# A three-step gated graph network on 64 graphs: host-laid inputs, one accumulating gate bank in two copies, and a new order in the first frame

## The reference

```
a  = A h                      (the same A for "in" and "out")
z  = sigmoid(W3 [a, a] + b_w3 + U3 h + b_u3)
r  = sigmoid(W4 [a, a] + b_w4 + U3 h + b_u3)
hv = tanh(W5 [a, a] + b_w5 + U5 (r * h) + b_u5)
h  = (1 - z) * h + z * hv
```

## Time and profile before

| | |
|---|---|
| median of 3 runs | 770.13 us (769.85 to 770.3) |
| the profiled execution | 770.7 us, of it the span 768.7 us |
| mean granted TensorE clock | 0.992 of full speed |
| PE busy | 752.5 us (98%), 3722 matmuls |
| DVE, ACT, POOL busy | 612.0, 438.8, 67.3 us |
| DMA | 52.15 MB in 285234 packets, 267386 of them under 512 B |

### The profile page before, as it was taken

The page is one execution under the profiler, slowest core; times in us unless marked ns, Lnnn a source line. Parts: engine busy times, 40 slices in busy tenths (PEclk is TensorE's granted clock), DMA queues, the critical chain, the costliest instruction groups (busy, mean ns, idle before and its releaser), DMA issues.

```text
span 768.7 us, 10991 instructions
## 1 busy us (share of the span) xinstructions
PE 752.5 (98%) x3722; PEld 637.8 (83%) x3722; DVE 612.0 (80%) x969; ACT 438.8 (57%) x745; POOL 67.3 (9%) x91
## 2 busy tenths in 40 slices
PE   7999999999999999999999999999999999999994
PEld 6888888888888888888888888888888888888883
DVE  3787688868997778787988777888789867888785
ACT  3565555556766555555666655555567655555564
POOL 0000012100000011110010001120000000211003
PEclk9999999999999999999999999999999999999997
DMA  7811642122265372222156336222225632221223
GB/s 188 144 29 28 104 76 38 30 37 40 39 130 123 66 131 42 32 39 40 29 114 118 71 76 120 38 37 33 37 39 117 138 64 38 32 32 32 43 36 112
DMA packets 285234, 52.15 MB, mean 68 GB/s; under 512 B 267386, under 2 KB 284420, under 8 KB 285188
## 3 DMA queue, kind: packets, MB, share of 16 engines
q1 hardware_dynamic: 284916, 51.24, 35.8%
q10 hardware_dynamic: 272, 0.26, 0.1%
HBM read 18.95 MB, written 8.39 MB: 36 GB/s over the span
## 4 chain that ended last, share of the span: by engine, by line
PE 95%; DVE 2%; DMA 1%; issue 1%; ACT 1%; POOL 0%; ACTq 0%; SPq 0%; POOLq 0%; DVEq 0%
PE ps_a L353 11%; PE ps_uz L328 11%; PE ps_uz L329 11%; PE ps_uz L330 11%; PE ps_v L328 11%; PE ps_v L330 11%; PE ps_v L329 11%; PE ps_r L328 6%; PE ps_r L330 6%; PE ps_r L329 6%; DMA x_in<-in_x 1%; PE ps_uz L426 0%; DVE dz L647 0%; DVE hT L657 0%; DVE stats L757 0%
## 5 line engine op out<-in xcount | busy, mean ns | idle before, releaser
L519 ACT ACTIVATE ps_v<-ps_v,bias 128x512 f32<-128x512 f32 x96 | 63.6, 662 | 73.0 <-PE ps_v L330 73.0
L642 DVE TENSOR_TENSOR dz<-ps_v,hT 128x512 f32<-128x512 f32 x64 | 44.2, 691 | 76.4 <-ACT ps_v L519 76.4
L543 ACT ACTIVATE ps_r<-ps_r,bias 128x512 f32<-128x512 f32 x96 | 63.5, 662 | 71.1 <-DVE ps_r L663 70.2
L514 ACT COPY u_sb<-ps_uz 128x512 f32<-128x512 f32 x96 | 56.4, 587 | 73.5 <-PE ps_uz L330 73.5
L501 ACT CAST aT_hi<-ps_a 128x512 fp32r<-128x512 f32 x96 | 56.1, 586 | 65.5 <-PE ps_a L353 65.4
L328 PE MATMUL ps_uz<-hT_hi,wt_lo 128*128 128x512 f32 x192 | 79.1, 412 | 0.0
L552 ACT CAST rh_hi<-rh 128x512 fp32r<-128x512 f32 x96 | 59.6, 621 | 28.2 <-DVE rh L668 28.2
L329 PE MATMUL ps_uz<-hT_lo,wt_hi 128*128 128x512 f32 x192 | 75.1, 391 | 0.0
L330 PE MATMUL ps_uz<-hT_hi,wt_hi 128*128 128x512 f32 x192 | 75.0, 391 | 0.0
L328 PE MATMUL ps_uz<-aT_hi,wt_lo 128*128 128x512 f32 x192 | 74.9, 390 | 0.0
L328 PE MATMUL ps_r<-aT_hi,wt_lo 128*128 128x512 f32 x192 | 74.9, 390 | 0.0
(11 more groups left out here) (84 smaller groups left out, 1564.8 us busy)
## 6 DMA issues: line engine op xcount, KB each, us to landing
hn<-hb SPq DMA_DIRECT2D x736, 32.0 KB, 2.0
x_in<-in_x SPq DMA_DIRECT2D x16, 512.0 KB, 5.0
x_blk<-in_x SPq DMA_DIRECT2D x64, 128.0 KB, 3.7
out<-y SPq DMA_DIRECT2D x15, 512.0 KB, 3.0
wide<-in_L_gnn_w_w SPq DMA_DIRECT2D x3, 512.0 KB, 4.2
out<-y SPq DMA_DIRECT2D x2, 256.0 KB, 2.1
square<-in_L_gnn_u_w ACTq DMA_DIRECT2D x1, 256.0 KB, 3.3
square<-in_L_gnn_u_w SPq DMA_DIRECT2D x1, 256.0 KB, 4.6
```

Source lines behind the costliest of these rows:

```text
L514: nc.scalar.copy(u_sb[:, oc, :], ps_uz[:, oc, :]).then_inc(u_copied, 1)
L519: nc.scalar.activation(ps_v[:, oc, :], ps_v[:, oc, :], ACT.Tanh, bias=bias[:, BV, oc:oc + 1]).then_inc(v_ready, 1)
L543: nc.scalar.activation(ps_r[:, oc, :], ps_r[:, oc, :], ACT.Sigmoid, bias=bias[:, BR, oc:oc + 1]).then_inc(r_ready, 1)
L642: nc.vector.tensor_tensor(dz[:, c, :], ps_v[:, c, :], h_of(j)[:, c, :], ALU.subtract).then_inc(d_ready, 1)
```

## The change

- The host hands over other layouts: `x` nodes first and also features first, the adjacency and all weights transposed, the biases as one features-first array; the output is written nodes first and turned on the host. PE's 22 transposes of weights, adjacency and biases go, and so do `load_blocks`, `transpose_x` and their buffers. `xT` is loaded directly (`load_cols`, 512 KB in runs of 2 KB).
- `xT` of the next round is loaded by SP right behind `move` of the slot's last frame (frames 8 to 11); before, `load_blocks` stood in `load`, ahead of `load_rows`.
- u, W4 a and then (W3 - W4) a are accumulated in one bank pair `ps_g[j % 2]`: sigmoid(u + W4 a) is read for r between them, and the third product turns the sum into u + W3 a for z. `copy_u` and `add_u` go. The sigmoid for r writes to SBUF (`r_sb`). W3 - W4 is made once (`subtract_r`).
- PE's frame order becomes `gate_r`, `value`, `gate_z`; `gate_z` waits for the sigmoid of r, and `u_product` waits for the z of two frames before, not one. On ACT the two `rh_hi` casts come before the two z sigmoids; on DVE `times_r` comes before `h_low`.
- The first frame has its own order on all engines (`first=True`), 24 and 8 warm-up transposes in place of 10 and 26, and x and weights loaded in another order.

```diff
 (SP)
-            def load_blocks(i, q):
-                for f in range(QUADS):
-                    sp.dma_start(x_blk[q % 2][f * BLK:(f + 1) * BLK, :, :, :],
-                                 x_blocks[f, :, :, bass.ds((SLOTS * i + q) * NBLK, NBLK), :])\
-                      .then_inc(blocks_loaded[q % 2], DMA)
+            def load_cols(i, q, c=slice(0, C)):
+                sp.dma_start(xT[q][:, c, :], x_cols[:, bass.ds(SLOTS * i + q, 1), c, :].rearrange("p g c r -> p (g c) r")).then_inc(xT_loaded[q], DMA)
...
             def load(i, q):
                 oi, oq = (i, q - 2) if q >= 2 else (i - 1, q + 2)
-                sp.wait_ge(xT_ready[oq], oi + 1)
-                load_blocks(i, q)
                 sp.wait_ge(a_ready, 2 * frames(oi, oq))
                 load_rows(i, q)
...
                 if carry or j > 0:
-                    move(*frame_before(i, j))
+                    bi, bj = frame_before(i, j)
+                    move(bi, bj)
+                    if refill and bj >= FR - SLOTS:
+                        load_cols(bi + 1, bj % SLOTS)
...
+            sp.dma_start(adjT[:, :], adj_t).then_inc(adjT_loaded, DMA)
             load_rows(0, 0)
-            load_blocks(0, 0)
...
+            for c in range(C):
+                load_cols(0, 0, slice(c, c + 1))
+            load_wide(W4)
+            load_wide(W5)
+            load_wide(W3)
             load_rows(0, 1)
+            load_cols(0, 1)
+            sp.dma_start(square[1][:, :, :], u5_t).then_inc(w_loaded[U5], DMA)
+            load_cols(0, 2)
+            load_cols(0, 3)
 (PE)
-                    dense(ps_uz, U3, oc, hT_hi, hT_lo, True, True).then_inc(u_ready, 1)
+                    dense(ps_g[j % 2], U3, oc, hT_hi, hT_lo, True, False)
...
-                pe.wait_ge(z_ready, C * frames(*frame_before(i, j)))
+                if carry or j >= 2:
+                    pe.wait_ge(z_ready, C * frames(*two_before(i, j)))
...
-                    dense(ps_r, W4, oc, aT_hi, aT_lo, True, True).then_inc(rpre_ready, 1)
+                    dense(ps_g[j % 2], W4, oc, aT_hi, aT_lo, False, True).then_inc(rpre_ready, 1)
...
-                    pe.wait_ge(u_copied, C * frames(i, j) - 1 + oc)
-                    dense(ps_uz, W3, oc, aT_hi, aT_lo, False, True).then_inc(zpre_ready, 1)
+                    pe.wait_ge(r_ready, C * frames(i, j) - 1 + oc)
+                    dense(ps_g[j % 2], W3, oc, aT_hi, aT_lo, False, True).then_inc(zpre_ready, 1)
...
                 gate_r(i, j)
+                value(i, j, carry)
                 gate_z(i, j)
-                value(i, j, carry)
...
-                keep_warm(10)
-                pe.wait_ge(adj_loaded, DMA)
-                nc.tensor.transpose(adj_bank, adj_in[:, :], ident[:, :]).then_inc(adj_transposed, 1)
-                transpose_weight(U3)
-                pe.wait_ge(adjT_ready, 1)
+                keep_warm(24)
+                pe.wait_ge(adjT_loaded, DMA)
                 aggregate(0, 0)
-                keep_warm(26)
+                keep_warm(8)
                 weight_ready(U3)
-                u_product(0, 0, between=transpose_weight)
...
+                u_product(0, 0)
                 weight_ready(W4)
                 gate_r(0, 0)
+                weight_ready(W5)
+                value(0, 0, False)
                 weight_ready(W3)
                 gate_z(0, 0)
...
+                first_half(0, 1, False)
                 weight_ready(U5)
-                first_half(0, 1)
                 candidate(0, 0)
 (ACT, frame)
                 for oc in range(C):
-                    if following:
+                    if following and not first:
                         h_high(*following, oc)
-                    act.wait_ge(rsum_ready, C * frames(i, j) - 1 + oc)
-                    nc.scalar.activation(ps_r[:, oc, :], ps_r[:, oc, :], ACT.Sigmoid,
+                    act.wait_ge(rpre_ready, C * frames(i, j) - 1 + oc)
+                    nc.scalar.activation(r_sb[:, oc, :], ps_g[j % 2][:, oc, :], ACT.Sigmoid,
                                          bias=bias[:, BR, oc:oc + 1]).then_inc(r_ready, 1)
+                    if first and oc == 0:
+                        weight_high(W3)
+                for oc in range(C):
+                    act.wait_ge(rh_ready, C * frames(i, j) - 1 + oc)
+                    nc.scalar.copy(rh_hi[:, oc, :], rh[:, oc, :]).then_inc(rh_hi_ready, 1)
                 for oc in range(C):
                     act.wait_ge(zpre_ready, C * frames(i, j) - 1 + oc)
...
-                    act.wait_ge(rh_ready, C * frames(i, j) - 1 + oc)
-                    nc.scalar.copy(rh_hi[:, oc, :], rh[:, oc, :]).then_inc(rh_hi_ready, 1)
+                if first:
+                    for oc in range(C):
+                        h_high(*following, oc)
+                    weight_high(U5)
 (DVE, frame)
-                add_u(i, j, 0)
-                if before:
                     new_h(bi, bj, 1)
-                add_u(i, j, 1)
                 for c in range(C):
-                    if following:
+                    times_r(i, j, c)
+                    if first and c == 0:
+                        weight_low(W3)
+                    if following and not first:
                         h_low(*following, c)
-                    times_r(i, j, c)
                 rh_low(i, j, 0)
                 rh_low(i, j, 1)
+                if first:
+                    for c in range(C):
+                        h_low(*following, c)
+                    weight_low(U5)
...
+            def subtract_r():
+                dve.wait_ge(wsum_ready, SUMMED[W3] - 1)
+                nc.vector.tensor_tensor(wsum[W3][:, :, :], wsum[W3][:, :, :], wsum[W4][:, :, :],
+                                        ALU.subtract).then_inc(wsum_ready, 1)
```

More of the change, by code:

```diff
@@ L92, in build @@
         neg_half = sb("neg_half", [P, GB])
-        wide = [sb(f"wide{k}", [P, C, 2 * D]) for k in range(3)]
+        wide = [sb(f"wide{k}", [P, 2, C, D]) for k in range(3)]
         square = [sb(f"square{k}", [P, C, D]) for k in range(2)]
@@ L134, in build @@
         dz = sb("dz", [P, C, ROWS])
-        ps_v, ps_uz, ps_a, ps_r = ps("ps_v"), ps("ps_uz"), ps("ps_a"), ps("ps_r")
+        ps_v, ps_a = ps("ps_v"), ps("ps_a")
+        ps_g = [ps(f"ps_g{k}") for k in range(2)]
         def f32(t):
@@ L271, in store, with frame @@
                              y[q % 2][:, :, :]).then_inc(stored[q % 2], DMA)
-            def frame(i, j, carry):
+            def frame(i, j, carry, refill):
                 if j < 2:
@@ L306, in _ @@
                 for j in range(EARLY, FR):
-                    frame(i - 1, j, True)
+                    frame(i - 1, j, True, True)
                 for j in range(EARLY):
-                    frame(i, j, True)
+                    frame(i, j, True, True)
             last = ROUNDS - 1
             for j in range(EARLY, FR - 1):
-                frame(last, j, True)
+                frame(last, j, True, False)
             for q in range(SLOTS - 1):
@@ L355, in aggregate, with u_product @@
                     done.then_inc(a_ready, 1)
-            def u_product(i, j, between=None):
+            def u_product(i, j):
                 pe.wait_ge(hT_hi_ready, C * frames(i, j))
@@ L485, in _ @@
             candidate(last, FR - 1)
+            pe.wait_ge(z_ready, C * frames(last, FR - 2))
             for c in range(C):
                 pe.wait_ge(h_ready, C * frames(last, FR - 1) - 1 + c)
-                output(SLOTS - 1, c, ps_r)
+                output(SLOTS - 1, c, ps_g[0])
         @block.scalar
@@ L509, in h_high @@
                 nc.scalar.copy(hT_hi[:, c, :], h_of(j)[:, c, :]).then_inc(hT_hi_ready, 1)
-            def copy_u(i, j):
-                for oc in range(C):
-                    act.wait_ge(u_ready, C * frames(i, j) - 1 + oc)
-                    nc.scalar.copy(u_sb[:, oc, :], ps_uz[:, oc, :]).then_inc(u_copied, 1)
             def tanh_v(i, j):
@@ L529, in normalise, with frame @@
                                          scale=rstd[q][:, b:b + 1]).then_inc(normed[q], 1)
-            def frame(i, j, carry, following):
+            def frame(i, j, carry, following, first=False):
                 if carry or j > 0:
@@ L618, in statistics @@
                     nc.vector.bn_aggr(meanvar[q][:, b, :], stats[q][:, b, :]).then_inc(meanvar_ready[q], 1)
-            def transpose_x(i, q):
-                dve.wait_ge(blocks_loaded[q % 2], QUADS * DMA * turn(i, q))
-                nc.vector.transpose(xT[q][:, :, :].rearrange("p c r -> p (c r)"),
-                                    x_blk[q % 2][:, :, :, :].rearrange("p c k f -> p (c k f)")).then_inc(xT_ready[q], 1)
             def transpose_blocks(i, j, again):
@@ L680, in h_low, with frame @@
                                         ALU.subtract).then_inc(hT_lo_ready, 1)
-            def frame(i, j, carry, following):
+            def frame(i, j, carry, following, first=False):
                 before = carry or j > 0
```

(10 more changed lines are left out.)

170 lines of the change are left out of this document (67 added, 103 removed).

## The result

| | before | changed |
|---|---|---|
| median of the runs | 770.05 us (4 runs, 769.85 to 770.3) | 763.06 us (4 runs, 762.16 to 763.5) |
| ratio to before, 95% interval | | 0.9908 (0.989 to 0.9925) |
| the profiled execution, its span | 770.7, 768.7 us | 762.16, 760.4 us |
| first U3 h, U3 h of frame (0, 1) | 14.34, 29.71 us | 8.76, 22.63 us |
| from there to the start of DVE's last `v_minus_h` (its first half) | 726.18 us | 725.26 us |

7.0 us less between the medians, and 8.3 us less span between the two profiled executions. The changed one is the fastest of its runs; the same kernel profiled again had a span of 761.3 us and a median of 763.38 over 5 runs. Where the 8.3 us are: 29.71 - 22.63 = 7.08 in the opening, 726.18 - 725.26 = 0.92 up to the last `v_minus_h`, and 0.3 in what follows it.

What follows compares the result with a forecast made beforehand. PE, holding 95% of the last-ending chain, was taken as the bound, so only the edges could gain: 770.7 - 5.15 (opening) - 0.9 (end) = 764.65 us, forecast 764.1 for the median; range of 8 in 10, 762.4 to 767.7.

Steps and rivals of the forecast that it cites:

- The frame: Steady-state rounds: frames stay 15.40 us apart, PE does not wait, and every added wait costs 0.
- gate z on r: New wait of gate z for r's sigmoid in each frame: 1.35 us of margin in the worst frames, cost 0.
- The slower rival: Rounds: xT's refill behind move comes late and stalls PE; 1 us in each of 12 frames gives 776; chance 0.05.
- The landing of xT: Opening: xT of slot 0 lands at 8.6 us, the middle of 6.7 and 10.5.
- PE's own path: Opening: 24 warm-ups, the aggregation and 8 warm-ups end at 10.1 us; the data decides, U3 h starting at 10.65.
- U3 h at 9.3: Opening, early end of the forecast: PE-bound, gain 6.5 us there; with 0.9 at the end, 762.7 us.
- Everything behind it: First frame after U3 h at 10.65: four products, aggregation and a 1.0 us stall, U3 h of (0, 1) at 24.55.
- Two thirds from x and the warm-ups that no longer fill the gap: Opening: two thirds of its 5.15 us gain come from features-first x and those warm-ups, the smaller part from the transposes.
- The end: Last v_minus_h: DVE's statistics start over 1 us earlier and the tanh decides, 0.9 us gained, bounds 0 and 0.95.
- The sum: Whole kernel: 770.7 - 5.15 - 0.9 = 764.65 us, then 0.57 lower for the median, 764.1.
- The clock rival: Opening: PE falls to half clock after idling, costing 1.5 to 2 us, 765.9 us in all; chance 0.08.
- The rival of late loads: Opening: the slowest DMA engine sets each landing, xT at 10.2 and W3 at 17.1 us; 767.3 us; chance 0.16.

Runs made afterwards that it cites:

- e2: The changed kernel with gate z directly behind gate r again, ahead of value; 783.75 us, ratio 1.0178.
- e4: The changed kernel without its 24 and 8 warm-up transposes; 763.27 us, ratio 0.9915.
- e3: The changed kernel with x_in read from the reference's own layout, in runs of 1 KB and not 4 KB; 763.31 us, ratio 0.9925.
- e7: The changed kernel with xT loaded in 128-byte runs, one DMA per chunk, still features first; 765.31 us, ratio 0.994.
- e1: The changed kernel with ACT's two casts of h of frame (0, 1) ahead of the first frame's z sigmoids; 761.97 us, twice.
- e8: e1 with xT of slot 0 loaded ahead of x_in and without the 8 later warm-ups; 767.74 us, ratio 0.9969.
- e9: e8 with 48 warm-ups in front in place of 24; 763.28 us, ratio 0.9916.
- e10: e1 without the 8 warm-ups behind the first aggregation, loads in the changed kernel's order; 765.07 us, ratio 0.9937.
- e6: The changed kernel with the accumulating bank taken back: u copied and added, gate z before value, W3 itself; 765.17 us, ratio 0.9941.

## Why the prediction was right

It forecast 764.1 us and 763.06 was measured, a gain of 7.0 where 6.0 had been worked out. In the second trace, 763.05 us and so near the median, U3 h of (0, 1) comes at 23.52, 1.0 us before the 24.55 forecast, as much as the forecast of the median is off. Step by step:

- **The frame.** 15.40 us and no wait of PE in the rounds, as said, with every added wait at cost 0. The one that I thought nearest, gate z on r, was the nearest: 1.49 us of margin against 1.35 forecast, and e2 shows its price when the margin is gone, 19 us of span and 20 in the medians. The slower rival (xT's refill late) did not come: in the whole execution ACT waits once for a DMA into xT, 2.5 us, in the opening.
- **The landing of xT, the term that was mis-sized.** I took 8.6 us, the middle of 6.7 and 10.5, with the reason that it cannot be near the early end since x_in had landed at 7.94. It was cast at 6.67 and 7.56 in the two profiled executions. The early end was right and the reason against it wrong: the 7.94 was not a property of the loads that the new kernel has. e4 has x_in at 5.87, e3 and e7 by 6.24 and 6.44. The rate was the smaller matter: in the first trace the loads moved at 278 GB/s from 2 to 4 us and at 389 from 4 to 6, where I had used 293 throughout, and 293 gives the 6.7. e7, which gives xT 128-byte runs, casts at 9.28; why x_in was at 7.94 before stays open.
- **PE's own path, sized wrong too.** I had PE ready at 10.1, with 5.7 us for the 24 warm-ups; they took 4.79 and 5.38, and PE was ready as U3 h started, at 8.76 and 9.65. With 10.1 an earlier landing would have been worth only 0.5 us. The bound of the range, "U3 h at 9.3", did not go with the 10.1 of the step either, and 8.76 lies beyond it. Had PE needed the 10.1, half of the miss would have gone; that both paths were shorter than reckoned and met to within some tenths was not foreseen.
- **Everything behind it** was right: 13.90 us from the first U3 h to that of (0, 1) forecast, 13.87 measured, with the stall of 1.0 (0.92) from the order of z and the casts. e1 takes that stall away and gains it.
- **"Two thirds from x and the warm-ups that no longer fill the gap"** holds, for x above all: of the 7.08 us of the opening 5.58 lie ahead of the first U3 h (14.34 to 8.76). hT_lo is complete at 13.80 before and at 8.61 now, 5.19 earlier; the 26 warm-ups of the kernel before held U3 h only for the other 0.4. e4 says nothing on them, it takes out those of the changed kernel.
- **The end**, 0.9 forecast, 0.92 measured. But only 0.54 of it is the work removed from DVE; the rest was a longer pause of DVE in the traced execution of the kernel before, so the 0.92 is in part luck.
- **Outside the span** nothing was worked out. The sum kept the 2.0 us of the traced execution and took off 0.57 for the median; usual executions of the kernel before have 2.6 us there and the changed kernel 1.8. The 0.8 us gained there stands in no term of the sum. Inside the span usual executions gain 5.9 us, close to the 6.05 of the sum, but the sum started from a trace 1.5 us longer than usual and had the first U3 h 1.0 us too late: that these two nearly cancel is luck.
- **The clock rival** did not come as described: no window of the changed kernel's opening is at 0.50. Yet the aggregation took 2.09 us in the second trace and 1.79 in the first. e8 and e9 show that the rival was a real one. Its price was worked out at 1.5 to 2 us; it is about 1.6.
- **The rival of late loads** had xT at 10.2 and W3 at 17.1 us. xT was there at 6.67, and the three wide weights landed 5.4 to 7.0 us after their issue, so the last by 11.3.

## What to carry to other kernels

When one engine is full in the steady state, taking work off the others pays only at the two ends of the kernel (1.3 us of span here, of 99 us of busy time that the banks removed from DVE and ACT; another 0.8 us outside the span came with them, for a reason not found), and what such a rework may cost is read from its new waits: measure how far each released value lies ahead of the instruction that wants it, in the worst frames, and put independent work between. An opening has two paths, the landing of the first operand with the casts behind it, and what stands ahead on PE; work out both, and do not take a landing over from a kernel with another queue. And compare a trace with the spans of the other executions before taking a difference from it. Last, a small edit of straight-line code ahead of a loop was followed here by 3.8 us of pauses in places that it does not touch (e10), so look at the loop's ends in the new trace.

## What the hardware showed that I had not expected

- The "instruction" queue moved 14 packets in e4 and 33 or 34 in every other kernel; 32 warm-ups ahead of the loop are the whole difference between e4 and the changed kernel, which has 34.
- The PE pauses without a releaser at the starts of rounds 2 and 3: 1.86 and 1.38 us in e10 with 0.3 each in the frame after, 3.1 us in all in e8, 0.9 in e2, 0.1 us or less in the other kernels.
- The granted clock is not readable in the first microseconds: in e4 the windows from 6 to 9 us say 1.00 while 16 aggregation matmuls take 3.75 us against 1.78 at full clock; the same holds for the first 24 warm-ups (4.79 to 5.38 us, some 0.2 us each, against 0.11 for each of the 8 later ones).
- Order in the queue costs its issues and its bytes: x_in lands at 5.87 us as SP's second load (e4) and at 8.63 as its fourth (e8). Of the 2.8 us, 0.94 are its later issue (1.32 and 2.26), and 1.8 the time from issue to landing (4.55 and 6.37 us) with 0.52 MB more ahead of it, some 290 GB/s.
- The time outside the span differs by kernel: 1.7 to 2.1 us in every execution of the kernels with the accumulating banks, 2.65 to 3.09 in e6 and 2.6 in the median of the kernel before, which do without them.
